# Issuing the second layer's gathers two by two, with a wait for the landing of each pair

## The reference, cut to what matters

```python
h = jnp.maximum(_layernorm(x, axis=-1), 0.0)
x = x + _L1_gnn_ref(h, edge_index, L1_gnn_W, L1_gnn_b)
# inside _L1_gnn_ref:
row, col = (edge_index[0], edge_index[1])
neigh = jax.ops.segment_sum(x[row], col, num_segments=n)
count = jax.ops.segment_sum(jnp.ones_like(col, dtype=x.dtype), col, num_segments=n)
neigh = neigh / jnp.where(count == 0, 1.0, count)[:, None]
out = jnp.concatenate([x, neigh], axis=-1) @ W + b
```

## Time and profile before

| what | us |
|---|---|
| median of the runs shown (3) | 10293.0 |
| lowest and highest of them | 10287.89, 10295.07 |
| span of the profiled execution, first to last instruction | 10335.9 |
| from the first gather of the changed line to the last | 2563.6 to 4076.4 |

### The profile page before, as it was taken

One profiled execution on the slowest core, in us unless ns is written; L12 is line 12 of the kernel. 1 busy time (PEld: TensorE's weight loads), 2 busy tenths in 40 slices (PEclk: granted clock), 3 DMA queues, 4 the chain that ended last, 5 costly groups with the idle time before them and its releaser, 6 DMA issues. The chain is left out here.

```text
span 10335.9 us, 115065 instructions
## 1 busy us (share of the span) xinstructions
PE 4876.0 (47%) x30691; PEld 3800.3 (37%) x30691; DVE 5676.5 (55%) x16123; ACT 2431.2 (24%) x4069; POOL 5859.2 (57%) x5314
## 2 busy tenths in 40 slices
PE   6888888884666666334444444444467000000000
PEld 3554455442556555234444444444465000000000
DVE  7888888885666666245555555555576212212221
ACT  0111111111333333134444444444453000000000
POOL 5888888884333333444444444444423666666665
PEclk8888888886777877555555555555555555555555
DMA  3333333332000000233333333333331111111111
GB/s 78 35 35 35 35 35 35 35 30 59 20 16 14 15 15 20 46 57 63 64 65 63 63 66 63 64 64 63 64 89 51 46 47 47 46 47 47 46 49 43
DMA packets 927382, 484.76 MB, mean 47 GB/s; under 512 B 828205, under 2 KB 842007, under 8 KB 925218
## 3 DMA queue, kind: packets, MB, share of 16 engines
q0 software_dynamic: 309120, 199.89, 16.7%
q1 hardware_dynamic: 615872, 277.33, 10.0%
q10 hardware_dynamic: 2304, 6.55, 0.2%
HBM read 218.57 MB, written 185.20 MB: 39 GB/s over the span
## 5 line engine op out<-in xcount | busy, mean ns | idle before, releaser
L2099 POOL DMA_INDIRECT tile_rows<-att_row_table,src_by_tile x1612 | 1588.2, 985 | 1676.4 <-ACT tags_l L2117 1181.3
L892 POOL DMA_INDIRECT acc<-val,idx x1240 | 1918.6, 1547 | 416.9 <-issue 372.2
L1142 POOL DMA_INDIRECT rows_l<-relation_table,idx x1612 | 1528.3, 948 | 758.0 <-issue 481.8
L2212 PE MATMUL banks<-rows_l,prob 128*128 128x65 f32 x4032 | 790.2, 376 | 1464.7 <-ACT piece_part L2150 1438.5
L1155 DVE SCALAR_TENSOR_TENSOR run<-run,mask,rows_l 128x64 f32<-128x64 f32 x1612 | 460.8, 286 | 1813.0 <-issue 1332.6
L2212 PEld LDWEIGHTS banks<-rows_l,prob 128*128 128x128 f32 x4032 | 752.3, 287 | 1524.8 <-ACT prob L2144 1233.3
L701 PE MATMUL banks<-part 128*128 128x490 bf16 (+1 forms) x5580 | 1296.6, 392 | 0.0
L1293 POOL DMA_INDIRECT gathered_rows<-h_table,gathered_index x600 | 567.9, 947 | 952.0 <-ACT gathered_index L1403 784.1
L1191 PE MATMUL banks<-run,link 128*128 128x64 f32 x98 | 21.9, 414 | 2299.8 <-PEq L1122 2289.0
L2263 DVE TENSOR_TENSOR banks<-banks,piece_att_dst 128x1024 f32<-128x1024 f32 x252 | 312.2, 1239 | 1436.2 <-remote 1301.6
L1191 PEld LDWEIGHTS banks<-run,link 128*128 128x128 f32 x98 | 21.5, 329 | 2299.5 <-issue 2299.5
(11 more groups left out here) (397 smaller groups left out, 9777.5 us busy)
## 6 DMA issues: line engine op xcount, KB each, us to landing
rows_l<-tile_rows SPq DMA_DIRECT2D x2016, 38.5 KB
piece_sums<-kept_l SPq DMA_DIRECT2D x252, 264.0 KB
running_sums<-run SPq DMA_DIRECT2D x62, 832.0 KB
attr<-in_edge_attr SPq DMA_DIRECT2D x61, 624.0 KB
tile_rows<-att_row_table,src_by_tile POOLq DMA_INDIRECT x1612
rows_l<-relation_table,idx POOLq DMA_INDIRECT x1612
acc<-val,idx POOLq DMA_INDIRECT x1240
gathered_rows<-h_table,gathered_index POOLq DMA_INDIRECT x600
```

Source lines behind the costliest of these rows:

```text
L892: e.indirect_dma_start(acc_d[k], bass.IndirectOffsetOnAxis(ap=idx[h][:, r:r + 1], axis=0), val[h][:, r, :], None, compute_op=ALU.add).then ...
L1142: e.indirect_dma_start(gbuf[h][:, r, :], None, table, bass.IndirectOffsetOnAxis(ap=idx[h][:, r:r + 1], axis=0))\
L2099: e.indirect_dma_start(gathered[:, g % TRING, r, :], None, hx_d, bass.IndirectOffsetOnAxis(ap=src_col[:, t:t + 1], axis=0))\
L2212: last = e.matmul(ps[5 + r // GROUP][:, r % GROUP * W1:(r % GROUP + 1) * W1], prob[u % 2][:, r, :], rows[u][:, r, 0:W1], start=True, stop= ...
```

## The change

In `gather`, ahead of the third, fifth, seventh, ninth and eleventh gather of a turn, POOL waits until the gathers issued so far in this turn have landed, and adds one to the counter `s_gpace`. `s_grow[s]` stands at i x 16 x 12 before the turn's first gather, and each gather adds 16. Order, number, targets and indices of the gathers stay, and so do the instructions of all other engines.

```diff
                         for u in range(GP):
+                            if u and u % 2 == 0:
+                                e.wait_ge(s_grow[s], i * 16 * GP + 16 * u)
+                                e.sem_inc(s_gpace, 1)
                             e.indirect_dma_start(grow[s][:, u, :], None, h1_d,
                                                  bass.IndirectOffsetOnAxis(ap=gidx[s][:, u:u + 1], axis=0))\
                              .then_inc(s_grow[s], 16)
```

## The result

| | before | after |
|---|---|---|
| median of 4 executions each, us | 10290.4 | 10033.1 |
| lowest and highest | 10285.7, 10295.1 | 10029.5, 10040.7 |
| the profiled execution: span | 10335.9 | 10038.9 |

The ratio is 0.975 (95% interval 0.974 to 0.976): 2.5% faster, 257 us, at 10033 us where 10025 was predicted. The profiled execution of after took 10040.65 us, 1.8 us more than its span.

What follows compares the result with a forecast made beforehand. Engines starved of instructions by a backlog of shared work behind POOL's second-layer gathers were taken as the bound; 24 pairs x (61.2 - 50) = 269 us off 10293 gave 10025 us, range 9900 to 10310.

Steps and rivals of the forecast that it cites:

- The bound: Second layer: PE and other engines starved of instructions beside POOL's gathers; starved turns cost 470 us.
- The total, 50 us a pair: Second layer: a pair of turns falls from 61.2 to 50 us, 24 pairs, 269 us saved.
- POOL's two groups: POOL's gathers in a pair of second-layer turns take 45.6 us, at 1.55 us for each added wait.
- The engines' own pace: Second layer at full instruction supply, corrected for granted clock: 22.4 us a turn, 45 us a pair.
- What starvation is left: Second layer with paced gathers: from no starvation, 46 us a pair, to slow refill, 56 us; 50 taken.
- rival D: Second layer, full relief: 46 us a pair, 365 us faster, 9930 us; chance 0.68 together with the main case.
- The waits are free on the path: POOL's second-layer waits are hidden by over 30 us of slack, up to 3.1 us a wait.
- Rival C: POOL becomes the second layer's bound at over 3.1 us a wait; 211 us slower at 4 us; shared chance 0.18.
- A, a place in the code: Stall sits at a code place, not with the gathers: no change, within 20 us of 10293; 0.14 including partial gains.
- B, starving as long as any gather is in flight: Second-layer engines starve with any gather in flight, however few: 370 us slower, 10660 us; shared chance 0.18.
- The argument from the median: Profiled span is only 43 us above the runs' median, so 470 us of starvation can't belong to the profiled execution alone.
- The signs named beforehand: Second layer: slow turn 25 to 30 us, gather pairs about 4 us apart, ACT's b0b wait under 250 us.

Runs made afterwards that it cites:

- nogather: Kernel before with the second layer's gathers left out, row buffers zeroed, third-layer counts checked; 9766.3 us against 10288.4 on starving chip 15 (ratio 0.949).
- pairs_again: The changed kernel again, waits after every second gather, plus bounds checks on third-layer counts; 8648.8 us against 8400.7 for the kernel before on chip 11.
- by6: Changed kernel with one wait a turn, after the sixth gather, plus third-layer count checks; 8407.4 us against 8400.7 for the kernel before on chip 11.
- by3: Changed kernel waiting after every third gather, with count checks; 8448.2 us against 8400.7 on chip 11, 9896.6 against 10285.9 on starving chip 4.
- by4: Changed kernel waiting after every fourth gather, with count checks; 8410.9 us against 8400.7 on chip 11, 9960.8 against 10285.9 on starving chip 4.

## Why the prediction came out as it did, point by point

**The bound.** Right that the gathers hold the other engines back, and by how much. It was inferred from where ACT's and DVE's b0b waits and PE's "issue" stood; nogather shows it, and 49 x (30.2 - 20.3) = 485 us of starvation stand against the 470 of the prediction. "Starved of instructions" is more than the runs show: that engines are late without a wait is seen, that a fetch is late is not.

**The total, 50 us a pair.** Measured 50.3 in the loop. The sum 24 x (61.2 - 50) = 269 us stands against 272 us in the stage. But its three terms were all off, and that the total is right is luck, because they cancelled:
- *POOL's two groups*, taken as 45.6 us with 1.55 us a wait: they take 49.5, as a wait costs 1.94. The value lies outside its own bounds of 1.35 to 1.75. The row used for it has DVE at the end of the wait, 2.60 us from the gather's start; POOL itself goes on only 3.19 us after it. The landing is not what is longer: it comes at 2.4 us (the page of pairs_again, where the step is 3.2 us too), so POOL takes some 0.8 us from the landing to the next gather's start, of which 0.30 stand ahead of every gather. The 2.60 us and the 0 to 0.4 "to get going" had left 0.2 to 0.6 for this.
- *The engines' own pace*, taken as 22.4 us a turn, 45 a pair: it is 20.3 with gathers and 19.6 without. The correction by the clock was the error: I carried the first layer's granted clock of 0.84 over, where by6 is granted 0.96. With 0.96 the same formula gives 19.4 / (0.92 + 0.08 / 1.73) = 20.1 us.
- *What starvation is left*, taken as 4 us a pair between the bounds of none and 10: none that shows, as the turn of 25.1 us is the same on a chip that doesn't starve. The refill is fast enough at its lower bound or better, and rival D was right in this.

**"The waits are free on the path."** This is the step that failed. It compared two groups, 45.6 us, with the old pair of 61.2, and gave up to 3.1 us a wait. But the change itself takes the pair to what the engines need, 40.6 us, and against that two groups never fitted. From then on each wait is paid in full: after lost 25.1 - 20.3 = 4.8 us a turn to POOL, 230 us in 48 turns, nearly as much as it won. Rival C named this with the right sign of PE waiting ahead of the gathered product and POOL going from turn to turn without a pause, only at a price of over 3.1 us; the price at which it decides was mis-set, for the reason just given. With a turn of 20.3 us POOL bounds it from (20.3 - 15.0) / 5 = 1.06 us a wait.

**Rivals.** A, a place in the code, fell with nogather and with the chips that don't starve on the same code. B, starving as long as any gather is in flight, fell with the change itself: POOL has a gather in flight for some 3.7 of each 4.44 us, and next to no load is late.

The Trainium skill (Runtime: NRT & Kernel Launch, section Instruction fetch mechanics) calls the instruction stream hidden unless a branch breaks it. The prediction says that the trace disagrees, and that reading doesn't hold: steps of 0.7 us are seen, but no instruction packet beside them. On chips 11 and 2 nothing speaks against the page either: from 2700 to 3500 us PE's loads stand behind "issue" for 13.8 us in by6, never over 0.2 us at a time, where in the kernel before it is 287.9 us, up to 9.6 at a time. The Trainium skill (DMA: Bandwidth & Descriptors, section Anatomy of one DMA) puts about 2 us of fixed cost on a DMA that POOL issues; by the prediction's estimate from it a group would have been 19.8 us, and it measured 24.77.

**The argument from the median.** "They can't belong to the profiled execution alone" was weaker than it read. Every time here, 10033.1 and 8400.7 alike, comes from an execution with a recorded span some 2 us below it, so whether a starving chip also starves when nothing is recorded is open, and the incomplete records of these chips make it a question to be asked. What I didn't think of at all is that it might belong to the chip: the chance of slower, 0.18, held no such case, and on two of the four chips of the experiments slower is what the change is.

**The signs named beforehand.** The slow turn at 25 to 30 us: 25.0. Pairs about 4 us apart and 21 to 24 us a group: 4.44 and 24.7. The b0b wait under 250: gone. POOL's idle time at the landings, other stages unchanged: so.

## What to carry to other kernels

When the waits ahead of several engines are "issue" or a long-finished DMA, and they come a few microseconds after a long unbroken row of indirect DMAs, break the row up, by time rather than by landings where that can be done, and over the seams between groups as well. Pairs with some 1.1 us more between them saved 4.0% here; threes and fours with landing waits saved 3.8% and 3.2%, and cost 0.5% and 0.1% where there was nothing to relieve. Price a wait on the engine that is to wait, and set its cover against the pace that the change itself will bring, not against the old one. Compare the kernel before on several chips first, and look whether the landings are all in the record: the sign of such a change can hang on the chip, and perhaps on the recording.

## What the runs showed of the hardware that was not expected

- Two of the four numbered chips starve beside gathers and two don't: the kernel before takes 10288.4 and 10285.9 us or 8400.7 and 8402.1 us, 22% apart, at the same duration of every instruction looked at (944 ns a gather, 286 and 285 ns a DVE step). What sets them apart, the chip, what its other cores do, how the program lies in memory or how the record is taken, no run tells; the starving ones are those whose record lacks more than half of the semaphore updates.
- On the starving ones, in the rows shown, late loads begin 4.4 to 5.7 us after the first of an unbroken row, and end 9.5 us after it for six, 12.5 for eight and 16.4 to 17.1 (medians) for twelve.
- A gather that POOL waits for lets it go on 3.19 us after its start, on both sorts of chip, 1.94 us later than without the wait; its landing is at 2.4 us.
- Not tried: the kernels without a recorded span; a wait or a pause ahead of a turn's first gather too, which would break the seams of by3 and by4, and pauses without a landing in the third and the last layer, where DVE's chain (L1155) still goes by steps of 0.7 and 1.4 us.
